# A graph layer: part of the key softmax moved from the opening into the edge loop, and bias products joined

## The reference

```python
edge_index = jnp.stack([src, dst])
xn = _layernorm(x, axis=-1)
x = x + gnn(xn, edge_attr_20, ..., edge_index) + mix(xn[None], ...)[0]
x = x + ffn(_layernorm(x, axis=-1)[None], ...)[0]
return x

def gnn(x, rbf, ...):            # row, col = ei
    filt = jax.nn.silu(rbf @ Wf1 + bf1) @ Wf2 + bf2
    agg = jax.ops.segment_sum(x[col] * filt, row, num_segments=x.shape[0])
    h = jax.nn.silu(agg @ Wu1 + bu1) @ Wu2 + bu2
    ...                           # batch norm of h, added to x

def mix(x, ...):                  # 8 heads of 32
    q, k, v = ...                 # x @ Wqkv
    k = jax.nn.softmax(k, axis=1) # over the nodes
    context = jnp.einsum('bnhd,bnhv->bhdv', k, v)
    out = jnp.einsum('bnhd,bhdv->bnhv', q, context).reshape(b, n, c)
    hgate = jax.nn.gelu(xn @ Wg1 + bg1, approximate=False)
    gate = jax.nn.sigmoid(hgate @ Wg2 + bg2)
    return out * gate @ Wproj + bproj
```

## Time and profile before

| | |
|---|---|
| runs | 2213.65, 2218.55, 2227.55 us |
| profiled execution | 2221.49 us, span 2219.7 us |
| PE busy | 1924.0 us, 87% |
| POOL busy | 1441.2 us, 65% |
| DVE busy | 1528.4 us, 69% |
| ACT busy | 1307.3 us, 59% |
| opening | to 189.67 us |
| scatters | 212.13 to 1702.39 us |

### The profile page before, as it was taken

One profiled execution on the slowest core, in us unless ns is written; L12 is line 12 of the kernel. 1 busy time (PEld: TensorE's weight loads), 2 busy tenths in 40 slices (PEclk: granted clock), 3 DMA queues, 4 the chain that ended last, 5 costly groups with the idle time before them and its releaser, 6 DMA issues. The chain is left out here.

```text
span 2219.7 us, 38972 instructions
## 1 busy us (share of the span) xinstructions
PE 1924.0 (87%) x10218; PEld 1587.5 (72%) x10218; DVE 1528.4 (69%) x3525; ACT 1307.3 (59%) x2330; POOL 1441.2 (65%) x989
## 2 busy tenths in 40 slices
PE   3687999989999989998899989998990785999878
PEld 2466788778877777777777777777780574788678
DVE  6654777777767767776776677767771557999645
ACT  2333776767666667666776676667760463666423
POOL 2111888888888888888888888888885550455300
PEclk9898999999999999999999999999995895999979
DMA  8656888988898888888988888798886880000002
GB/s 276 275 225 204 160 157 153 187 147 149 146 180 155 149 157 169 145 153 158 171 155 151 173 160 155 141 184 156 143 132 121 263 277 0 1 0 0 20 20 97
DMA packets 288441, 325.45 MB, mean 147 GB/s; under 512 B 29575, under 2 KB 251178, under 8 KB 288146
## 3 DMA queue, kind: packets, MB, share of 16 engines
q0 software_dynamic: 112896, 102.81, 37.7%
q1 hardware_dynamic: 169568, 216.13, 30.9%
q10 hardware_dynamic: 5746, 3.90, 0.7%
HBM read 167.64 MB, written 154.97 MB: 145 GB/s over the span
## 5 line engine op out<-in xcount | busy, mean ns | idle before, releaser
L903 POOL DMA_INDIRECT sums<-summed,out_idx x784 | 1238.8, 1580 | 295.7 <-issue 208.3
L957 PE MATMUL bank<-wf,hidT 128*128 128x256 f32 x3136 | 802.0, 384 | 0.0
L957 PEld LDWEIGHTS bank<-wf,hidT 128*128 128x128 f32 x3136 | 547.2, 192 | 54.7
L1048 ACT ACTIVATE hidT<-bank,bf 128x512 f32<-128x512 f32 x392 | 269.8, 688 | 265.4 <-PE bank L935 222.3
L1143 DVE TENSOR_TENSOR msg_low<-msg,msg_high 128x512 fp32r<-128x512 f32 x392 | 271.9, 694 | 175.0 <-ACT msg_high L1068 129.0
L1174 DVE TENSOR_TENSOR msg<-bank,gathered 128x512 f32<-128x512 f32 x392 | 269.2, 687 | 117.6 <-PE bank L957 91.6
L1068 ACT ACTIVATE msg_high<-msg 128x512 fp32r<-128x512 f32 x392 | 247.3, 631 | 92.2 <-DVE msg L1174 79.1
L955 PE MATMUL bank<-gnn_bf_halves,ones 128*128 128x256 f32 x784 | 298.2, 380 | 0.0
L1056 ACT ACTIVATE summed<-pair 128x516 f32<-128x516 f32 x392 | 230.3, 588 | 61.6 <-DMA sums<-summed,out_idx 59.1
L1075 ACT ACTIVATE gathered<-bank 128x512 f32<-128x512 f32 x392 | 231.9, 592 | 49.8 <-issue 22.3
L945 PE MATMUL bank<-window,spread 128*128 128x256 f32 x784 | 194.6, 330 | 62.6 <-DVE spread L1138 38.3
(11 more groups left out here) (324 smaller groups left out, 2823.4 us busy)
## 6 DMA issues: line engine op xcount, KB each, us to landing
window<-xn_halves SPq DMA_DIRECT2D x392, 128.0 KB
sums<-gate SPq DMA_DIRECT2D x32, 800.0 KB, 10.1
id_row<-id_rows SPq DMA_DIRECT2D x98, 256.0 KB
attr<-attr_rows SPq DMA_DIRECT2D x98, 256.0 KB
part<-sums SPq DMA_DIRECT2D x48, 512.0 KB, 6.6
xn_halves<-xn_halves SPq DMA_DIRECT2D x7, 1792.0 KB, 6.6
id_row<-id_rows SPq DMA_DIRECT2D x98, 128.0 KB
sums<-summed,out_idx POOLq DMA_INDIRECT x784
```

The costliest lines, as they stand in the source:

```text
L903: nc.gpsimd.indirect_dma_start(g.sums_dram[k], bass.IndirectOffsetOnAxis(ap=out_idx[:, ET * c + t:ET * c + t + 1], axis=0), summed[c % 2][ ...
L957: mm = T.matmul(out, hidT[:, j // 2, f, ds((2 * (j % 2) + t) * P, P)], g.wf2[:, f, :], start=False, stop=f == CB - 1)
L1048: A.activation(hidT[:, h, f, :], hps[:], ACT.Silu, bias=g.bf1[:, f:f + 1]).then_inc(hid_ready, 1)
```

## The change

Three things. **Key softmax and gram**: the opening keeps those of groups 0 to 3 (`EARLY = 4`). Groups 4 to 6 move into the first 14 chunks of the edge loop (`LEAD`), 56 pairs, by a second function of places, `prepare(q, place)`, with 18 places a group (`LATE_PLACES`). There the work has two banks instead of five, so ACT first copies the keys into `e_col`, which shares its space with `gate`; maxima and exponentials are taken from that copy. The rows of x are not in memory any more: SyncE loads them again into `res_stage`, and VectorE normalises them again. **The fold** goes to places 54 of this stretch and 1 and 3 of the output of group 0. **The output** of the seven groups has 12 chunks each (48 places) instead of 14. Last, **bias products**: one product of 512 columns for both tiles of a pair takes the place of two of 256, in `filt`, in the projection and in the last stage.

```diff
+EARLY = 4
+LEAD = 14
+LATE_PLACES = 18
+AT_KEYS = (0, 1, 2, 3)
+AT_EXP = (6, 7)
+AT_ROWS = (5, 6, 7, 8)
+AT_TURN = (8, 10, 12, 14)
+AT_GRAM = (10, 12, 14, 16)
+AT_ADD = 17
+AT_FOLD = 54
+AT_CTX, AT_WQM = 1, 3
-PLACES = 4 * 14
+PLACES = 4 * 12
...
# opening, TensorE (VectorE and ACT likewise)
-                if k:
+                if 1 <= k <= EARLY:
                     turn_e(k - 1)
-                k_product(k)
+                if k < EARLY:
+                    k_product(k)
...
-                else:
+                elif k <= EARLY:
                     gram_group(k - 1)
-            turn_e(NG - 1)
-            gram_group(NG - 1)
...
# edge loop
+    def along(eng, chunk, prepare, output):
+        for n in range(LEAD):
+            chunk(n // 2, n % 2, False, lambda q: prepare(*divmod(4 * n + q, LATE_PLACES)))
...
# SyncE
+            def prepare(q, place):
+                if place == 0 and q < NG - EARLY:
+                    k = EARLY + q
+                    n = GT - 1 if k == NG - 1 else GT
+                    if q:
+                        sp.wait_ge(gram_made, k)
+                    sp.dma_start(res[:, 0:n, :], split_rows(g.x_dram, k * GT, n)).then_inc(x_in, 16)
...
# TensorE
+            def keys(q, j):
+                k, h, f = EARLY + q, j // CB, j % CB
+                if j >= 2:
+                    pe.wait_ge(keys_copied, 4 * q + j - 1)
+                elif q and j == 0:
+                    pe.wait_ge(e_ready, 4 * k)
+                elif q:
+                    pe.wait_ge(gram_added, k)
+                for b in range(CB):
+                    mm = T.matmul(bankKeys[j % 2][:, 0:HC], g.wqkv[:, b, ds(C + f * P, P)],
+                                  g.xT[:, b, ds(k * GC + h * HC, HC)], start=b == 0, stop=b == CB - 1)
+                mm.then_inc(k_made, 1)
...
+            def prepare(q, place):
+                if q * LATE_PLACES + place == AT_FOLD:
+                    fold(0)
+                elif q < NG - EARLY:
+                    if place in AT_KEYS:
+                        keys(q, AT_KEYS.index(place))
+                    if place in AT_TURN:
+                        turn_e(q, AT_TURN.index(place))
+                    if place in AT_GRAM:
+                        gram_rows(q, AT_GRAM.index(place))
...
# ACT
+            def copy_keys(q, j):
+                h, f = j // CB, j % CB
+                n = tokens_in(EARLY + q, h)
...
+                A.activation(e_col[:, f, ds(h * HC, n)], bankKeys[j % 2][:, 0:n], ACT.Copy).then_inc(keys_copied, 1)
+
+            def expo(q, h):
+                k = EARLY + q
+                if h == 0:
+                    act.wait_ge(maxed, k + 1)
+                    act.wait_ge(keys_copied, 4 * q + 4)
+                    act.wait_ge(sum_step, SUM_STEPS * (k - 1))
+                    A.activation(fade[k % 2][:], fade_log[:], ACT.Exp).then_inc(faded, 1)
+                for f in range(CB):
+                    cols = e_col[:, f, ds(h * HC, tokens_in(k, h))]
+                    A.activation(cols, cols, ACT.Exp, bias=g.neg_max[k % 2][:, f:f + 1],
+                                 accum_out=k_part[k % 2][:, f, h:h + 1]).then_inc(k_exp, 1)
...
# VectorE
+                elif q < NG - EARLY:
+                    if place - 2 in AT_KEYS:
+                        maximum(q, AT_KEYS.index(place - 2))
+                    if place - 2 == AT_KEYS[-1]:
+                        maxima(q)
+                    if place in AT_ROWS:
+                        normalise_rows(q, AT_ROWS.index(place))
+                    if place - 1 in AT_TURN:
+                        copy_e(q, AT_TURN.index(place - 1))
+                    if place == AT_ADD:
+                        add_group(q)
...
# last stage
-                nc.tensor.matmul(out, g.ones2[:], g.b_out[:], start=True, stop=False)
+                if u % 2 == 0:
+                    n = min(2, NT - u)
+                    nc.tensor.matmul(yps[u // 2 % 8][:, 0:n * C], g.ones2[:], for_tiles(g.b_out, n), start=True, stop=False)
```

More of the change, by code:

```diff
@@ L168, in opening @@
     neg_group = sb("neg_group", [P, CB], F32)
-    neg_max = [sb(f"neg_k_max{k}", [P, CB], F32) for k in range(2)]
     fade_log = sb("fade_log", [P, CB], F32)
@@ new lines, in turn_e @@
+            def turn_e(q, n):
+                k = EARLY + q
+                pe.wait_ge(k_exp, 4 * k + (2 if n == 0 else 4))
+                if n:
+                    pe.wait_ge(e_ready, 4 * k + n)
+                for i, t in enumerate(pair_tiles(n)):
+                    rows = rows_of(k * GT + t)
+                    for f in range(CB):
+                        mm = T.transpose(bankT[0:rows, ds((i * CB + f) * P, P)], e_col[:, f, ds(t * P, rows)], g.ident[:])
+                mm.then_inc(e_turned, 1)
@@ new lines, in gram_rows @@
+            def gram_rows(q, n):
+                k = EARLY + q
+                pe.wait_ge(e_ready, 4 * k + n + 1)
+                pe.wait_ge(presum_ready, 4 * q + n + 1)
+                for t in pair_tiles(n):
+                    rows = rows_of(k * GT + t)
+                    for f in range(CB):
+                        mm = T.matmul(bankK[:, ds(f * C, C)], e_node[0:rows, t, ds(f * P, P)], res[0:rows, t, :],
+                                      start=t == 0 and f == 0, stop=t == GT - 1 and f == CB - 1, skip_group_check=True)
+                if n == 3:
+                    mm.then_inc(gram_made, 1)
@@ new lines, in fold @@
+            def fold(k):
+                if k == 0:
+                    pe.wait_ge(gram_added, NG)
+                    for f in range(CB):
+                        for b in range(CB):
+                            mm = T.transpose(bankT[:, ds(b * C + f * P, P)], g.gram_acc[:, f, ds(b * P, P)], g.ident[:])
+                if k == 1:
+                    pe.wait_ge(fold_ready, FOLD_DONE + 2)
+                    for f in range(CB):
+                        for b in range(CB):
+                            mm = T.matmul(bankK[:, ds(f * P, P)], gram[:, b, ds(f * P, P)],
+                                          g.wqkv[:, b, ds(2 * C + f * P, P)], start=b == 0, stop=b == CB - 1)
+                if k == 2:
+                    pe.wait_ge(fold_ready, FOLD_DONE + 2 + CB)
+                    for b in range(CB):
+                        for f in range(CB):
+                            mm = T.matmul(bankT[:, ds(b * C + f * P, P)], g.wq_t[:, f, ds(b * P, P)], ctx_m[:, f, :],
+                                          start=True, stop=True)
+                mm.then_inc(mat, 1)
@@ L999, in output @@
             def output(s, place):
+                if is_first(s) and place in (AT_CTX, AT_WQM):
+                    fold(1 if place == AT_CTX else 2)
                 if place in AT_HIDDEN:
@@ new lines, in normalise_rows @@
+            def normalise_rows(q, n):
+                if n == 0:
+                    dve.wait_ge(x_in, 16 * (q + 1) + (16 if EARLY + q == NG - 1 else 0))
+                for t in pair_tiles(n):
+                    u = (EARLY + q) * GT + t
+                    rows = rows_of(u)
+                    op = V.tensor_scalar(res[0:rows, t, :], res[0:rows, t, :], g.mom.mean[0:rows, u:u + 1],
+                                         g.mom.rstd[0:rows, u:u + 1], ALU.subtract, ALU.mult)
+                op.then_inc(presum_ready, 1)
@@ new lines, in output @@
+            def output(s, place):
+                if is_first(s) and place == AT_CTX + 1:
+                    dve.wait_ge(mat, MAT_DONE + 2)
+                    dve.wait_ge(fold_ready, FOLD_DONE + 1)
+                    for f in range(CB):
+                        V.scalar_tensor_tensor(out=ctx_m[:, f, :], in0=bankK[:, ds(f * P, P)], scalar=k_inv[:, f:f + 1],
+                                               in1=g.head_mask[:], op0=ALU.mult, op1=ALU.mult).then_inc(fold_ready, 1)
+                if is_first(s) and place == AT_WQM + 1:
+                    dve.wait_ge(mat, MAT_DONE + 3)
+                    V.tensor_copy(g.wqm[:], bankT[:].rearrange("p (b n) -> p b n", b=CB)).then_inc(fold_ready, 1)
```

202 lines of the change are left out of this document (124 added, 78 removed).

## The result

The changed kernel takes 2247.05 us (median of four runs, 2241.10 to 2252.55) against 2219.87 for the one before in the same session: a ratio of 1.012, 95% interval 1.0075 to 1.0166. It is 27 us slower, where +9 was forecast, and lies 4 us above the range. The profiled executions have spans of 2250.8 and 2219.7, so 31.1 us are to be placed; the execution profiled after the change is the slowest of its four runs (2252.55), so the profiles overstate the loss by some 4 us.

What follows compares the result with a forecast made beforehand. The edge loop was taken as bound by POOL's scatters, 3.80 us a pair, TensorE next. Opening -10.0, late groups +18.1, fold +1.0 and joins -0.2 gave +8.9: 2227.4 us by the median, range 2208 to 2243 for 8 in 10.

Steps and rivals of the forecast that it cites:

- Opening, -10.0: Before the edge loop: earlier halves, full SyncE queue at 404 GB/s, fold gone; opening ends at 179.7 instead of 189.67.
- Late groups on TensorE, 232.5 us: First 56 pairs: TensorE needs 204.9 us of work plus 27.6 of waits from pair 0 to pair 56.
- From there to the scatter of pair 56, 6.8 us: First late stretch: delay from TensorE's product to its scatter, taken from the first pair, puts pair 56's scatter at 239.3.
- +18.1: First 56 pairs: scatter of pair 56 comes 239.3 us after TensorE's product of pair 0, instead of 221.2.
- "Twelve chunks instead of fourteen ... covered by POOL": Output groups after the late stretch: TensorE takes 3.3 us a pair against POOL's 3.8, so no cost.
- the +1.0 for the fold: Pairs 57 and 59: two later fold steps of 1.04 us each, half hidden because the lead is still nothing.
- Joins, -0.2: Last stage: 24 joined bias products on TensorE's path save 0.01 us each.
- Hiding: Rival for the first 56 pairs: late work hides behind POOL, +18.1 becomes 0, total -9.2, 2209 us; chance 0.16.
- An opening not limited by the queue: Rival for the opening: -18.7 instead of -10.0, total +0.2, 2219 us, chance 0.08; with hiding 2201, 0.03.
- VectorE as the limit: Rival for late pairs: none of VectorE's work hides, 34.9 us instead of 10.5, total +33.3, 2252 us; chance 0.12.
- The time of 2243: Rival for late table loads: each holds ACT twice as long through a drain, 15.4 us more, total +24.3; chance 0.03.
- The two signs that were to tell a wrong prediction: 113th scatter under 214 or over 245 us after the first, or opening ending before 173 or after 186.

Runs made afterwards that it cites:

- The experiment with the clears: Changed kernel with the last ten table clears issued from ACT's queue instead of SyncE's: 2242.91 us, 1.0111 of the kernel before.
- few-rows kernel: Changed kernel with VectorE's late normalisation cut to two columns of one tile a place: 2241.99 us, 1.0103 of the kernel before.
- joins alone: Kernel before with only the bias products joined: 2220.93 us, 0.9994 of the kernel before.
- the control: Kernel before with the hardware loop over five of the seven output groups written out: 2223.80 us, 1.0012 of the kernel before.
- Short groups with no late work: Kernel before with 12 output chunks a group, first 14 chunks empty of output work: 2224.09 us, 1.0008; with the loop written out 2220.63, 0.999.
- removing the switches: Changed kernel with tanh in place of the late exponentials and the fade, so no late table loads: 2230.87 us, 1.0046 of the kernel before.

## Why the prediction was wrong, point by point

- **Opening, -10.0: right, in size and mechanism.** -10.2. Group 5's halves were issued at 145.58 (forecast 145.3), group 6's at 151.72 (151), gate_scale at 177.58 (177.9), the first loop transfer at 179.47 (179.7). The experiment with the clears agrees that bytes are the limit.
- **Late groups on TensorE, 232.5 us: right in the sum,** 429.35 - 195.33 = 234.0, **but by errors that cancel, which is luck.** The bare work was put too low: 204.9, but 234.0 less 18.7 of waits and 6.2 of low clock (5.2, and 1.0 at the start, where it is 0.61 over 195.33 to 198) is 209.1. The pairs themselves are 170 instead of 162.4, the late products a little cheaper than priced. The waits were put too high, 27.6 against 24.9. ACT's part: the first block lasts 229.11 - 224.53 = 4.6 instead of 4.0 us, yet the waits for `gathered` and `attr_parts` are 13.0 against 15.6; what was left out is the low clock, 5.2 for the three groups. The switches alone cost 16.5. VectorE's work was put at 10.5; the waits for `spread` are 4.7 and the few-rows kernel gains 2.9.
- **From there to the scatter of pair 56, 6.8 us: too small.** It was taken from the first pair; the measured one is 440.36 - 429.35 = 11.0. And the base was one scatter short: 223.0 us, not 221.2. So +18.1 came out as 440.36 - 195.33 - 223.0 = +22.0.
- **"Twelve chunks instead of fourteen ... covered by POOL", 0: this step failed,** and with it the forecast: the tail takes 19.1 us more by the profiles, of which the +1.0 for the fold was all that the sum held. I compared rates, 3.3 us a pair against 3.8, and so allowed for neither the return of the loop (5.4 us more on TensorE at the first of four, hidden before by a lead of 26 us or more and not looked at) nor the fact that the lead starts at 11 us and grows slowly. Writing the loop out takes 11 us off the time by the ratios, 14.9 off the tail by the profiles. What is left over the kernel before, 4.2, is not shown to be anything: the tails of two kernels with 14-chunk groups, joins alone and the control, are 4.6 and 2.5 longer than before as well. Short groups with no late work have 9.9 in the same place with the loop, and 4.3 without it.
- **Joins, -0.2: right,** nothing measurable.
- **The rivals.** Hiding fell: 14 long gaps. An opening not limited by the queue fell: 179.47, not 171. VectorE as the limit fell, its price of 33.3 too. The time of 2243 that was given for table loads that hold ACT twice as long lies close to the measured one by chance, as its mechanism is not there: in the row above the fade starts 1.29 us after the load, with no drain. Each load cost TensorE 16.5/12 = 1.4 us, of which 10.7/12 = 0.9 are waits and 5.2/12 = 0.4 the low clock. By the drain that the Trainium skill, page "ScalarE: Activation LUTs", section "What ACT_TABLE_LOAD costs", adds to each load, the switches would have cost about twice that, an estimate; the traces show no drain.
- **The signs named beforehand.** Long gaps of 15 to 20 us in the first 112: 21.2, the last at pair 43, none later than pair 60. Scatters of 1.54 to 1.58 "as before": wrong, the mean of the tail rose from 1.577 to 1.593. TensorE idle 2 and 3 us behind the exponentials: 1.97 and 0.97. The two signs that were to tell a wrong prediction stayed silent (113th scatter 236.9 us after the first, opening to 179.47), because both look only at the stretch before the tail, and the step that failed lies behind it.

By ratios, removing the switches gave 16 us and writing the loop out 11, against the 26.6 of the whole change. Each was removed alone; whether both gains add up in one kernel was not tried. If they do, the gain of 10 in the opening pays for the rest of the late work.

## What to carry to other kernels

Work that is moved beside a bounding engine is free only if the next engine stays ahead at every point, so look for the worst few pairs and for what a lead was hiding (loop returns, function switches), not at mean rates. Price stalls of TensorE with the slow clock that can follow them: behind the 1.97 us at 227.95 the next eight products took 1.4 us more, behind the 1.97 us at 238.6 nothing. Give the prediction a sign for every stretch that it calls free, not only for the one that it expects to cost. Take the lead from the trace as a quantity of its own: how long an engine waits for the bounding one to free a buffer tells how much of it is left.

## What the runs showed of the hardware that was not expected

**The return of a hardware loop costs TensorE about 5 us here:** 3.13 to 4.25 idle in the kernel after and 3.27 to 3.68 before, then the low clock; the pair takes 7.2 to 9.4 us instead of 2.9. The label `<-issue` alone does not tell it: the kernel after with its loop written out has 3.87 under it at 1158.24, in front of `merge` and with a lead of 32 us, where POOL holds TensorE up. The returns are told by their place, the first `gather` of a group. The Trainium skill, page "Runtime: NRT & Kernel Launch", section "Instruction fetch mechanics", says that a taken branch to a target outside what is loaded stalls the engine until it is fetched; the idle that ends by no engine agrees with it, but no run shows the fetch itself.

**The length of a scatter is not fixed.** Most take 1.54 us, some up to 2.06. In the tail the mean is 1.577 before, 1.593 in the kernel after, and 1.580 in the latter with its loop written out. In the tail of the kernel after 0.87 of the scatters above 1.56 us overlap VectorE's `msg_low` (two operands in SBUF), but 0.56 of the short ones; a row of POOL and one of VectorE beside it:

```profile
1245.46 2.02 POOL L905 DMA_INDIRECT sums<-summed,out_idx  x1 [0.30 <-issue]
```

```profile
1245.37 0.70 DVE L1251 TENSOR_TENSOR msg_low<-msg,msg_high 128x512 fp32r<-128x512 f32 x1 [0.36 <-ACT msg_high L1146]
```

The Trainium skill, page "GPSIMD Engine Reference", section "8. Key points", names contention for the SBUF interfaces with VectorE's instructions of two SBUF inputs. That fits the overlap, which is a correlation and not `msg_low`'s alone: `out_idx` overlaps 0.81 of the long and 0.38 of the short ones, and `same`, with two operands in SBUF too, 0.37 and 0.57, the other way round. Nor is it a rule: the next scatter, from 1247.78 on, has the next `msg_low` (at 1248.88) inside it and took 1.54, and no run moved `msg_low` alone. The mean of the tail is 1.569 to 1.588 in the seven kernels whose lead stays full and 1.586 to 1.594 in the nine whose lead does not. Whether the two are cause and effect was not tried.
